# Key and query projections as three products of rounded high and low parts

## The chip, the cores and the metric

The kernel runs on one core of a Trainium2 chip. The metric is the device time of one execution in microseconds (us). The profile has five engines: TensorE (PE, with its weight loads as PEld), VectorE (DVE), ScalarE (ACT), GpSimd (POOL) and SyncE (SP), which only issues transfers here.

## The reference, cut to what matters

Two blocks of cross attention, a small mixture of experts and a quantised feed-forward layer, over 128 sequences of 64 tokens with 128 channels, 16 heads of 8 channels:

```python
x = x + tanh(g_xattn[0]) * L0_xattn(layernorm(x), ctx_1024, ctx_1024, ...)
x = x + tanh(g_ffn[0])   * L0_ffn(layernorm(x), ...)          # 4 experts, gated per token
x = x + tanh(g_xattn[1]) * L1_xattn(layernorm(x), ctx_1024, ctx_1024, mask, ...)
x = x + tanh(g_ffn[1])   * L1_ffn(layernorm(x), ...)          # quantised, depthwise convolution

# inside each xattn, all in float32:
q = query @ Wq.T + bq ; k = key @ Wk.T + bk ; v = value @ Wv.T + bv
attn = softmax(q k^T / sqrt(8)) ; out = (attn v) @ Wo.T + bo
```

## The kernel before, in words

**Tiles and groups.** A tile is two sequences, 128 rows; there are T = 64 tiles, and the residual stream `x_all` stays in SBUF. Four tiles make a group (G = 4); what comes ahead of the scores is done once per group with 512 columns. The stages follow one another: attention of layer 0 (L = 0), experts, attention of layer 1 (L = 1), feed-forward.

**One step of attention.** Each engine runs its own loop over the steps t (`attention(L)` on each engine, L442 on GpSimd, and the functions of the same name on the others), with j = t mod 4 the place in the group. `run_tiles` writes the first 8 and the last few steps out and loops over the rest, 8 steps to a body; in written-out steps t is a Python integer, in the loop a register. A step mixes the work of several tiles, and each engine takes its instructions in this order, so that the order written is the schedule; semaphores bind the engines. In step t:

- TensorE: scores of tile t (in layer 1 products that put in the mask first; both wait until VectorE has subtracted the maxima of tile t-1, `sub_done`), `values` of t-2, `transpose_p` first half of t-1, `transpose_o` of t-3 (waits for `x_attn`, the residual of t-4), then one piece of front work by j, then `transpose_p` second half, `project_o` of t-3. `bank[PT]` is one bank for both halves of `transpose_p`; ScalarE must have copied the first before the second is written.
- Front work by j, all in `bank[FRONT]`: j = 3 transposes the normalised queries of group (t+5)/4, j = 0 projects K (L1315), j = 1 projects Q (L1318), j = 2 projects V (L1323).
- ScalarE: exponentials second half of t-1, `copy_p` first half of t-1 (L581), `copy_o` of t-3, exponentials first half of t, `copy_p` second half of t-1, then the copy of the front work: `copy_xn` at j = 3 (L593), `copy_k` at j = 0 (L596), `copy_q` at j = 1 (L599), `copy_v` at j = 2.
- VectorE: residual of t-4 (L891), LayerNorm statistics of t+12 (L918), row maxima of the scores of t (`smax`, L923), the aggregate of the statistics (L925), two subtractions of the maxima (`prob`, L932), then `divide` of t-2 (`rden` L897, `o_n` L900).
- GpSimd: at j = 0 the scale and shift of the group t+8 (L382), at j = 0 and 1 its normalisation (L406, L408), at j = 1, 2, 3 the expansions of K for the scores (`expand_k`, L411), in every step the output bias onto `x_all` (L444).

**Types.** The K and Q projections of before are float32 matmuls with 128 rows, 128 weight columns and 512 moving columns; the profile shows two weight loads and two matmuls for one. The experts and the convolution already use the scheme of three products: an operand is copied to a rounded type (`F32R`, high part), the rest is the difference to it (low part), and high x high + high x low + low x high is added up (L1427 to L1429). For experts ScalarE makes the high part of the normalised tokens (L675) and VectorE the low (`split_mx`, L1042). GpSimd makes the low part of the convolution's weights (`tap_lower`, L515).

**Queues.** SyncE loads the context `ctx_t` of a group when V of the group two before is done, into two buffers; this is not touched.

Of the kernel before, what the change touches and what calls it, by code (L numbers as in the profile page):

```python
# [14 lines left out]
P = 128  # L15
# [11 lines left out]
G = 4  # L27
# [18 lines left out]
def build(nc, a, out):  # L46

    with ExitStack() as ctx:
# [3 lines left out]
        def sem(name):  # L52
# [134 lines left out]
            k_mm k_ready kj_ready v_mm v_ready q_mm q_ready  # L187
# [113 lines left out]
        RELU_A = tuple(c for c in range(EC) if c not in RELU_V)  # L301

# [72 lines left out]
        def _(pool):  # L375
# [47 lines left out]

            def attention(L):
                def step(t, k, has):
# [8 lines left out]
                    if j > 0 and has(f):  # L434
# [5 lines left out]
                        for h in ((), (0,), (1,), (2, 3))[j]:  # L440
                            expand_k(1 - gpar, h)
                    if has(0):  # L442
# [69 lines left out]
            def tap_lower():  # L512
# [7 lines left out]
            run_tiles(pool, attention(0), 8, 0, first=0, before={  # L520
                T - 8: lambda: lead_in(experts, -3, -3, NG), T - 7: lambda: lead_in(experts, -2, -2, NG)}, **TILES8)
# [5 lines left out]
                1: tap_scales, 4: lambda: tap_weights(0), 6: lambda: tap_weights(1), 7: lambda: tap_weights(2)}, **TILES8)  # L527
# [36 lines left out]
        def _(act):  # L564
# [27 lines left out]
            def copy_xn(src):  # L592
                act.activation(xn_t[:], src, ACT.Copy).then_inc(s["xn_copied"], G)  # L593
# [16 lines left out]
            def attention(L, beside=()):  # L610
                beside = dict(beside)

                def step(t, k, has):
# [12 lines left out]
                    if j == 3 and has(5):  # L626
                        f = n + 5
                        wait(act, "xn_tr", f + G)
                        wait(act, "q_mm", f)
                        copy_xn(bank[FRONT])  # L630
# [113 lines left out]
            def first_groups():  # L744
# [9 lines left out]
                copy_xn(bank[PT])  # L754
# [11 lines left out]
                copy_xn(bank[FRONT])  # L766
# [5 lines left out]
                T - 2: lambda: (normalise(1, 1, (2, 3)), relu(0, 0, 0, bank[FRONT]))}), 5, 0, first=0, before={  # L772
                T - 8: lambda: scale_wo(1), T - 5: lambda: split_weights(0), T - 4: lambda: split_weights(1)}, **TILES8)
# [54 lines left out]
            def attention1_tail():  # L828
# [16 lines left out]
            run_tiles(act, attention1, 5, 0, first=0, before={  # L845
                T - 8: lambda: copy_tap(0), T - 7: lambda: copy_tap(1), T - 5: lambda: (copy_tap(2), normalise_tile(0)),
# [7 lines left out]
        def _(dve):  # L854
# [49 lines left out]
            def attention(L):  # L904
                def step(t, k, has):
# [30 lines left out]
                    if has(-2):  # L936
                        divide(n - 2, k)
                return step
# [335 lines left out]
        def _(pe):  # L1274
# [44 lines left out]

            def project_v(L, gp, dst):  # L1320
# [7 lines left out]
            def attention(L, beside=()):  # L1328
                beside = dict(beside)

                def step(t, k, has):
# [32 lines left out]
                    if j == 0 and has(4):  # L1364
                        pe.wait_ge(ctx_ld[1 - gpar], group_loads(n + 4, 1 - gpar))
                        wait(pe, "xn_copied", n + 4 + G)
                        project_k(L, 1 - gpar, bank[FRONT])
                    if j == 1 and has(3):
                        wait(pe, "k_ready", n + 3 + G)
                        project_q(L, bank[FRONT])  # L1370
# [337 lines left out]
```

## Time and profile before

| | |
|---|---|
| median of 3 runs | 1009.33 us (999.88 to 1013.99) |
| the profiled execution, timed | 1009.39 us |
| its span | 1007.6 us |
| instructions | 36351 |
| granted TensorE clock, mean | 0.988 |
| moved between HBM and the core | 21.49 MB, 21 GB/s |

The span goes from the first to the last instruction on the core; 1.8 us of the timed execution lie around it. Busy time of an engine leaves out register, branch and semaphore instructions. Matmuls are pipelined: one shown as 0.40 us can be followed by the next after 0.23 us, so that a busy TensorE is not one at its peak. The idle time of an engine is put down to what ended it (after `<-`). A row of busy time by window gives the stretch, its length, the busy us (x instructions) of PE, PEld, DVE, ACT and POOL in this order, then the granted clock, the DMA share and GB/s.

### The profile page before, as it was taken

How to read it: one execution, taken by the hardware profiler on the slowest of the kernel's cores; microseconds unless marked ns; L12 is line 12 of the kernel's file. 1: busy time of each engine (PE TensorE's matmuls, PEld its weight loads, DVE VectorE, ACT ScalarE, POOL GpSimd, SP SyncE). 2: the span in 40 equal slices, each digit the busy share in tenths (PEclk: the TensorE clock that was granted, in tenths of full speed). 3: DMA queues.
4: the chain of work that ended last, by engine and by line, in shares of the span. 5: the costliest groups of instructions: out<-in, count | busy, mean ns of one | idle time of the engine just before them, and what ended most of it. 6: DMA issues, size and time to landing. Idle time of an engine off the chain costs nothing.

```text
span 1007.6 us, 36351 instructions
## 1 busy us (share of the span) xinstructions
PE 958.8 (95%) x11842; PEld 743.9 (74%) x11842; DVE 846.0 (84%) x2411; ACT 741.9 (74%) x1653; POOL 584.5 (58%) x1230
## 2 busy tenths in 40 slices
PE   6999999999999999999999999999999899999997
PEld 2777777777789999998877676767776666777775
DVE  5888888889689989888887888888877789999997
ACT  4877787788687777775657777777778777777774
POOL 6454554545125556656886535454554288888884
PEclk9999999999699999999999999999999999999999
DMA  3401010100000000000000000000000000000001
GB/s 108 176 24 42 21 42 31 32 21 11 13 2 2 0 0 0 0 0 1 2 12 24 13 22 10 21 10 12 19 11 2 2 15 21 21 21 21 21 21 30
DMA packets 19359, 21.49 MB, mean 21 GB/s; under 512 B 3552, under 2 KB 12000, under 8 KB 19296
## 3 DMA queue, kind: packets, MB, share of 16 engines
q1 hardware_dynamic: 19296, 20.68, 6.6%
q8 instruction: 35, 0.57, 0.2%
q14 instruction: 28, 0.23, 0.1%
HBM read 16.48 MB, written 4.19 MB: 21 GB/s over the span
## 4 chain that ended last, share of the span: by engine, by line
PE 30%; POOL 13%; issue 7%; ACT 2%; DVE 1%; POOLq 1%; ACTq 0%; DVEq 0%
PE bank L1276 8%; PE bank L1299 6%; POOL ln_rs L271 4%; PE score L1353 4%; POOL hid_b L555 3%; PE bank L1414 2%; PE score L1345 2%; PE bank L1323 2%; POOL xdq L551 2%; PE bank L1315 1%; PE bank L1311 1%; PE bank L1318 1%; ACT prob_t L581 1%; POOL ln_nr L271 1%; POOL ln_ve L271 1%
## 5 line engine op out<-in xcount | busy, mean ns | idle before, releaser
L581 ACT ACTIVATE prob_t<-bank 128x512 f32<-128x512 f32 x256 | 152.8, 597 | 124.9 <-PE bank L1276 116.8
L923 DVE TENSOR_REDUCE smax<-score 128x16 f32<-128x1024 f32 x128 | 156.8, 1225 | 49.1 <-PE score L1353 38.0
L1276 PE MATMUL bank<-const,prob 128*128 128x128 f32 x1024 | 167.7, 287 | 15.7 <-ACT prob_t L581 15.7
L1299 PEld LDWEIGHTS bank<-vb,prob_t 128*64 128x64 f32 x4096 | 131.6, 139 | 50.3 <-issue 42.2
L932 DVE TENSOR_TENSOR prob<-score,smax 128x512 f32<-128x512 f32 x256 | 164.9, 686 | 1.3
L576 ACT ACTIVATE prob<-prob 128x512 f32<-128x512 f32 x256 | 161.2, 630 | 6.1 <-DVE prob L932 5.4
L1276 PEld LDWEIGHTS bank<-const,prob 128*128 128x128 f32 x1024 | 109.4, 142 | 69.9 <-issue 60.7
L1299 PE MATMUL bank<-vb,prob_t 128*64 128x18 f32 x4096 | 144.4, 213 | 0.0
L411 POOL TENSOR_SCALAR kj<-k_sb,const 128x512 f32<-128x512 f32 x128 | 88.1, 695 | 74.8 <-issue 46.3
L656 ACT ACTIVATE eb_t<-eb,gwt 128x128 f32<-128x128 f32 x256 | 81.4, 390 | 45.2 <-POOL eb_acc L454 29.0
L382 POOL TENSOR_TENSOR a_ve<-a_mv,const 128x4 f32<-128x4 f32 x32 | 6.5, 203 | 147.9 <-DVE a_mv L925 143.8
L1353 PE MATMUL score<-kj,q_sb 32*64 32x256 f32 x2048 | 90.4, 409 | 1.8 <-ACT q_sb L599 0.9
L1555 PE MATMUL score<-f_wk_hi,tap_hi 128*128 128x512 f32 x192 | 81.8, 426 | 1.9 <-issue 1.8
L1556 PE MATMUL score<-f_wk_lo,tap_hi 128*128 128x512 f32 x192 | 75.7, 394 | 0.0
L1557 PE MATMUL score<-f_wk_hi,tap_lo 128*128 128x512 f32 x192 | 75.6, 394 | 0.0
L1414 PE MATMUL bank<-ew,hid_b 128*128 128x128 f32 x512 | 64.1, 280 | 2.5 <-DVE hid_b L1020 2.5
L1414 PEld LDWEIGHTS bank<-ew,hid_b 128*128 128x128 f32 x512 | 62.1, 196 | 4.5 <-issue 2.8
L1414 PE MATMUL bank<-ew,hid_a 128*128 128x128 f32 x512 | 62.8, 276 | 0.5 <-DVE x_all L1031 0.5
L1414 PEld LDWEIGHTS bank<-ew,hid_a 128*128 128x128 f32 x512 | 60.8, 192 | 3.0 <-DVE x_all L1031 0.9
L891 DVE TENSOR_TENSOR x_all<-bank,x_all 128x128 f32 (+1 forms) x128 | 37.2, 290 | 29.3 <-PE bank L1311 26.9
L444 POOL TENSOR_TENSOR x_all<-x_all,bo_row 128x128 f32 (+1 forms) x128 | 58.1, 457 | 0.0
L470 POOL TENSOR_TENSOR m_ve<-m_mv,const 128x4 f32<-128x4 f32 x16 | 3.3, 203 | 90.1 <-DVE m_mv L1054 86.1
(157 smaller groups left out, 2378.7 us busy)
## 6 DMA issues: line engine op xcount, KB each, us to landing
ctx_t<-in_ctx SPq DMA_DIRECT2D x32, 256.0 KB, 2.6
x_all<-in_x SPq DMA_DIRECT2D x16, 256.0 KB, 2.8
out_x<-x_all SPq DMA_DIRECT2D x64, 64.0 KB, 1.5
ew<-in_ew SPq DMA_DIRECT2D x2, 512.0 KB, 5.8
f_cw<-in_f_cw SPq DMA_DIRECT2D x1, 768.0 KB, 7.7
w_t<-in_w_attn SPq DMA_DIRECT2D x2, 256.0 KB, 3.8
f_w<-in_f_w SPq DMA_DIRECT2D x2, 256.0 KB, 6.5
eb<-in_L_ffn_eb SPq DMA_DIRECT2D x1, 256.0 KB, 6.5
```

The costliest lines, as they stand in the source:

```text
L411: pool.tensor_scalar(kj[:, gp, h, :], k_sb[:], const[:, C_J + h:C_J + h + 1], 0.0, ALU.mult, ALU.add).then_inc(s["kj_ready"], 1)
L576: act.activation(v, v, ACT.Exp, scale=SCALE).then_inc(s["exp_done"], 1)
L581: act.activation(prob_t[:, 4 * half:4 * half + 4, :].rearrange("p i q -> p (i q)"), bank[PT], ACT.Copy).then_inc(s["p_copied"], 1)
L656: act.activation(eb_t[:, j % 2, e, :], eb2[:, e * P:(e + 1) * P], ACT.Copy, scale=gwt[:, gp, j, e:e + 1]).then_inc(s["eb_mult"], 1)
L923: dve.tensor_reduce(smax[:].rearrange("p (r h) -> p r h", r=RH), sc, AX.X, ALU.max).then_inc(s["smax_done"], 1)
L932: dve.tensor_tensor(prob[:, par, half * 512:(half + 1) * 512].rearrange("p (r h k) -> p r h k", r=2, k=S), sc[:, g], m.unsqueeze(3).to_bro ...
L1276: return pe.transpose(dst, src, ident)
L1299: last = pe.matmul(bank[OV][q, i * 2 * VW:(i + 1) * 2 * VW], prob_t[:, i, q], vb[:, k // G, v0 + b * NPAIR + i, :, :].rearrange("p h v -> ...
L1353: last = pe.matmul(bank[r][q, 0:SW], q_sb[c, gpar, g], kj[c, gpar, :, g], start=(L == 0), stop=True, skip_group_check=True)
L1414: last = pe.matmul(bank[6 + j % 2][:, e * P:(e + 1) * P], hid[gpar][:, 2 * e + c, j * P:(j + 1) * P], ew2[:, 2 * e + c, :], start=(c == 0) ...
L1555: pe.matmul(bank[par], hi, f_wk_hi[:, tap, :], start=(tap == 0), stop=False)
L1556: pe.matmul(bank[par], hi, f_wk_lo[:, tap, :], start=False, stop=False)
```

## The change

Where K and Q are projected, the 512-column float32 product is replaced by three products of rounded operands, in every group but the first two of each layer (`whole(t, ...)` keeps these as they were). The high and low parts are formed thus:

- context: GpSimd multiplies `ctx_t` by one into `ctx_hi` and subtracts for `ctx_lo` (`split_ctx`), in its step j = 3, behind `expand_k` and ahead of the output bias. It waits for the loaded context, the K projection before, and its own high part.
- normalised queries: ScalarE's `copy_xn` writes the rounded `xn_hi` in place of `xn_t`; VectorE subtracts `xn_hi` from `bank[FRONT]` into `xn_lo`, at the end of its step j = 3, behind `divide`, waiting for `xn_copied`.
- weights: once per layer, ScalarE copies Wq and Wk to `w_hi` ahead of step 2, GpSimd subtracts for `w_lo` ahead of step 3.

TensorE waits for `ctx_lo_done` and `xn_lo_done` ahead of K. The parts lie in buffers of the experts and of the convolution that are free in attention, so no SBUF is added. The V projection stays float32 and reads `ctx_t`.

```diff
@@ -184,7 +184,7 @@
             tanh_done ident16_done wo_scaled setup_v mask_v vb_set thr_done zero_set edges_set
             sum_mm ffn_sum tern cw_scaled tap_ready tap_copied tap_split w2t_copied
             a_ln a_mean a_ready a_scaled a_xn_ready xn_tr xn_copied
-            k_mm k_ready kj_ready v_mm v_ready q_mm q_ready
+            k_mm k_ready kj_ready v_mm v_ready q_mm q_ready ctx_hi_done ctx_lo_done xn_lo_done w_hi_done w_lo_done
             scores_mm smax_done sub_done exp_done
             p_tr p_copied pv_mm rden_done o_norm o_tr o_copied wo_mm bo_added x_attn
             ln ln_mv ln_ready xn_ready
@@ -299,6 +299,19 @@
         GATE_STEPS = 16
         RELU_V = (1, 3, 7)
         RELU_A = tuple(c for c in range(EC) if c not in RELU_V)
+
+        ctx_hi, ctx_lo = mx_hi[:, 0, :], mx_lo[:, 0, :]
+        xn_hi, xn_lo = mx_hi[:, 1, :], mx_lo[:, 1, :]
+        w_hi = f_wk_hi[:, TAPS - 1, 0:2 * P].rearrange("p (w d) -> p w d", w=2)
+        w_lo = f_wk_lo[:, TAPS - 1, 0:2 * P].rearrange("p (w d) -> p w d", w=2)
+
+        def whole(t, first):
+
+            return isinstance(t, int) and t <= first
+
+        def parts_done(L, n):
+
+            return n - G - 2 * G * L
 
         block = ctx.enter_context(nc.Block())
 
@@ -421,6 +434,20 @@
                 for j in range(2):
                     normalise_pair(G, G, j)
 
+            def split_ctx(L, n, gp):
+                in_registers(pool, n, parts_done(L, n))
+                pool.wait_ge(s["const_in"], 16)
+                pool.wait_ge(ctx_ld[gp], group_loads(n, gp))
+                wait(pool, "k_mm", n)
+                pool.tensor_scalar(ctx_hi, ctx_t[:, gp, :], const[:, C_ONE:C_ONE + 1], 0.0, ALU.mult, ALU.add)\
+                    .then_inc(s["ctx_hi_done"], G)
+                wait(pool, "ctx_hi_done", parts_done(L, n))
+                pool.tensor_tensor(ctx_lo, ctx_t[:, gp, :], ctx_hi, ALU.subtract).then_inc(s["ctx_lo_done"], G)
+
+            def split_qk_weights(L):
+                pool.wait_ge(s["w_hi_done"], L + 1)
+                pool.tensor_tensor(w_lo, w_t[:, L, 0:2, :], w_hi, ALU.subtract).then_inc(s["w_lo_done"], 1)
+
             def attention(L):
                 def step(t, k, has):
                     n = L * T + t
@@ -439,6 +466,8 @@
                         wait(pool, "scores_mm", n + f - G)
                         for h in ((), (0,), (1,), (2, 3))[j]:
                             expand_k(1 - gpar, h)
+                    if j == 3 and has(5) and not whole(t, -1):
+                        split_ctx(L, n + 5, gpar)
                     if has(0):
                         wait(pool, "a_xn_ready", n + 1)
                         pool.tensor_tensor(x_tile(t), x_tile(t), bo_row[:, L, :], ALU.add)\
@@ -518,13 +547,14 @@
             first_groups()
             pool.wait_ge(s["setup_v"], 1)
             run_tiles(pool, attention(0), 8, 0, first=0, before={
+                3: lambda: split_qk_weights(0),
                 T - 8: lambda: lead_in(experts, -3, -3, NG), T - 7: lambda: lead_in(experts, -2, -2, NG)}, **TILES8)
             run_tiles(pool, experts, 3, 1, T=NG, first=-1, before={
                 NG - 3: lambda: (lead_in(attention1, -8, -5, mod=8), ternary(f_w1[:], 0)),
                 NG - 2: lambda: ternary(f_w2[:].rearrange("p c d -> p (c d)"), 1)})
             pool.wait_ge(s["setup_v"], 2)
             run_tiles(pool, attention1, 8, 0, first=0, before={
-                1: tap_scales, 4: lambda: tap_weights(0), 6: lambda: tap_weights(1), 7: lambda: tap_weights(2)}, **TILES8)
+                1: tap_scales, 3: lambda: split_qk_weights(1), 4: lambda: tap_weights(0), 6: lambda: tap_weights(1), 7: lambda: tap_weights(2)}, **TILES8)
 
             def ffn(t, par, has):
 
@@ -589,8 +619,12 @@
                                ACT.Identity, bias=b_col[:, L, 2:3])\
                     .then_inc(s["o_copied"], 1)
 
-            def copy_xn(src):
-                act.activation(xn_t[:], src, ACT.Copy).then_inc(s["xn_copied"], G)
+            def split_qk_weights(L):
+                act.wait_ge(s["w0_in" if L == 0 else "w1_in"], 16)
+                act.activation(w_hi, w_t[:, L, 0:2, :], ACT.Copy).then_inc(s["w_hi_done"], 1)
+
+            def copy_xn(src, dst):
+                act.activation(dst, src, ACT.Copy).then_inc(s["xn_copied"], G)
 
             def copy_k(L, src):
                 act.activation(k_sb[:], src, ACT.Identity, bias=b_col[:, L, 1:2]).then_inc(s["k_ready"], G)
@@ -627,7 +661,7 @@
                         f = n + 5
                         wait(act, "xn_tr", f + G)
                         wait(act, "q_mm", f)
-                        copy_xn(bank[FRONT])
+                        copy_xn(bank[FRONT], xn_t[:] if whole(t, -1) else xn_hi)
                     if j == 0 and has(4):
                         f = n + 4
                         wait(act, "k_mm", f + G)
@@ -751,7 +785,7 @@
                 act.wait_ge(s["k_mm"], G)
                 copy_k(0, bank[FRONT])
                 act.wait_ge(s["xn_tr"], G)
-                copy_xn(bank[PT])
+                copy_xn(bank[PT], xn_t[:])
                 act.wait_ge(s["q_mm"], G)
                 copy_q(0, 0, bank[OW])
                 act.wait_ge(s["g_in"], 32)
@@ -763,13 +797,14 @@
                 act.wait_ge(s["vb_set"], 3)
                 copy_v(0, bank[OV])
                 act.wait_ge(s["xn_tr"], 2 * G)
-                copy_xn(bank[FRONT])
+                copy_xn(bank[FRONT], xn_t[:])
 
             first_groups()
             run_tiles(act, attention(0, {
                 T - 7: lambda: normalise(0, 0, (0, 1)), T - 6: lambda: normalise(0, 0, (2, 3)),
                 T - 5: lambda: copy_mx(0, 0), T - 3: lambda: normalise(1, 1, (0, 1)),
                 T - 2: lambda: (normalise(1, 1, (2, 3)), relu(0, 0, 0, bank[FRONT]))}), 5, 0, first=0, before={
+                2: lambda: split_qk_weights(0),
                 T - 8: lambda: scale_wo(1), T - 5: lambda: split_weights(0), T - 4: lambda: split_weights(1)}, **TILES8)
             attention0_tail()
             run_tiles(act, experts, 2, 1, T=NG, first=1)
@@ -843,6 +878,7 @@
                 copy_xq(3, 1)
 
             run_tiles(act, attention1, 5, 0, first=0, before={
+                2: lambda: split_qk_weights(1),
                 T - 8: lambda: copy_tap(0), T - 7: lambda: copy_tap(1), T - 5: lambda: (copy_tap(2), normalise_tile(0)),
                 T - 4: lambda: (clear_edges(), normalise_tile(1)), T - 3: lambda: (quantise(0, 0), normalise_tile(2)),
                 T - 2: lambda: (quantise(1, 1), normalise_tile(3)), T - 1: copy_w2}, **TILES8)
@@ -935,6 +971,10 @@
                                 .then_inc(s["sub_done"], 1)
                     if has(-2):
                         divide(n - 2, k)
+                    if j == 3 and has(5) and not whole(t, -1):
+
+                        wait(dve, "xn_copied", n + 5 + G)
+                        dve.tensor_tensor(xn_lo, bank[FRONT], xn_hi, ALU.subtract).then_inc(s["xn_lo_done"], G)
                 return step
 
             def gate(ins):
@@ -1316,6 +1356,11 @@
 
             def project_q(L, dst):
                 pe.matmul(dst, w_t[:, L, 0, :], xn_t[:], start=True, stop=True).then_inc(s["q_mm"], G)
+
+            def project_parts(w, hi, lo, name):
+                pe.matmul(bank[FRONT], w_hi[:, w, :], hi, start=True, stop=False)
+                pe.matmul(bank[FRONT], w_hi[:, w, :], lo, start=False, stop=False)
+                pe.matmul(bank[FRONT], w_lo[:, w, :], hi, start=False, stop=True).then_inc(s[name], G)
 
             def project_v(L, gp, dst):
                 for i in range(G * BT):
@@ -1362,12 +1407,23 @@
                     if isinstance(t, int) and t in beside:
                         beside[t]()
                     if j == 0 and has(4):
-                        pe.wait_ge(ctx_ld[1 - gpar], group_loads(n + 4, 1 - gpar))
-                        wait(pe, "xn_copied", n + 4 + G)
-                        project_k(L, 1 - gpar, bank[FRONT])
+                        f = n + 4
+                        if whole(t, 0):
+                            pe.wait_ge(ctx_ld[1 - gpar], group_loads(f, 1 - gpar))
+                            wait(pe, "xn_copied", f + G)
+                            project_k(L, 1 - gpar, bank[FRONT])
+                        else:
+                            if isinstance(t, int):
+                                pe.wait_ge(s["w_lo_done"], L + 1)
+                            wait(pe, "ctx_lo_done", parts_done(L, f))
+                            wait(pe, "xn_lo_done", parts_done(L, f))
+                            project_parts(1, ctx_hi, ctx_lo, "k_mm")
                     if j == 1 and has(3):
                         wait(pe, "k_ready", n + 3 + G)
-                        project_q(L, bank[FRONT])
+                        if whole(t, 1):
+                            project_q(L, bank[FRONT])
+                        else:
+                            project_parts(0, xn_hi, xn_lo, "q_mm")
                     if j == 2 and has(2):
                         wait(pe, "q_ready", n + 2 + G)
                         project_v(L, 1 - gpar, bank[FRONT])
```

## Rows read from the trace of the kernel before

**Rows 1.** The page: busy time, share of the span and instructions of each engine

```profile
PE 958.8 (95%) x11842; PEld 743.9 (74%) x11842; DVE 846.0 (84%) x2411; ACT 741.9 (74%) x1653; POOL 584.5 (58%) x1230
```

**Rows 2.** Busy time by window: one group in layer 0, one in layer 1

```profile
98.21:114.50 16.29, 15.93 (x292) 11.89 (x276) 13.96 (x32) 12.99 (x27) 8.48 (x17) 1.00 0.11 32
...
604.87:622.25 17.38, 17.06 (x294) 12.34 (x292) 14.27 (x32) 12.89 (x26) 8.32 (x16) 1.00 0.05 15
```

**Rows 3.** Timeline (start us, us, engine), layer 0, the tile of a Q projection

```profile
104.09 1.02 PE L1318 MATMUL bank<-xn_t,w_t 128*128 128x512 f32 x2
...
104.24 0.60 ACT L581 ACTIVATE prob_t<-bank 128x512 f32<-128x512 f32 x1 [0.78 <-PE bank L1276]
...
104.95 0.42 PEld L1276 LDWEIGHTS bank<-const,prob 128*128 128x128 f32 x4 [0.67 <-issue]
```

**Rows 4.** Timeline, layer 0, from step j = 3 to the next tile

```profile
113.79 0.29 DVE L900 TENSOR_TENSOR o_n<-bank,rden 128x128 f32<-128x128 f32 x1
...
114.49 0.59 ACT L593 ACTIVATE xn_t<-bank 128x512 f32<-128x512 f32 x1
114.50 0.29 DVE L891 TENSOR_TENSOR x_all<-bank,x_all 128x128 f32 x1 [0.42 <-PE bank L1311]
...
115.41 1.23 DVE L923 TENSOR_REDUCE smax<-score 128x16 f32<-128x1024 f32 x1 [0.22 <-DVE a_st L918]
...
116.37 1.02 PE L1315 MATMUL bank<-ctx_t,w_t 128*128 128x512 f32 x2
...
118.21 0.69 PE L1353 MATMUL score<-kj,q_sb 32*64 32x256 f32 x16 [0.16 <-DVE prob L932]
...
118.56 0.29 DVE L891 TENSOR_TENSOR x_all<-bank,x_all 128x128 f32 x1
...
119.26 1.23 DVE L923 TENSOR_REDUCE smax<-score 128x16 f32<-128x1024 f32 x1 [0.21 <-DVE a_st L918]
```

**Rows 5.** Timeline, expert stage, TensorE: one product in three parts

```profile
402.01 0.48 PE L1427 MATMUL score<-mx_hi,ew_hi 128*128 128x512 f32 x1
402.33 0.40 PE L1428 MATMUL score<-mx_lo,ew_hi 128*128 128x512 f32 x1
402.56 0.39 PE L1429 MATMUL score<-mx_hi,ew_lo 128*128 128x512 f32 x1
```

**Rows 6.** Timeline, expert stage: the split of the normalised tokens

```profile
384.29 0.58 ACT L675 ACTIVATE mx_hi<-bank 128x512 fp32r<-128x512 f32 x1
...
384.91 0.69 DVE L1042 TENSOR_TENSOR mx_lo<-bank,mx_hi 128x512 fp32r<-128x512 f32 x1 [0.22 <-ACT mx_hi L675]
385.52 0.21 DVE L986 TENSOR_REDUCE g_rank<-g_gt 128x16 f32<-128x64 f32 x1
```

**Rows 7.** GpSimd: one line's instructions (ns min/median/max); timeline, layer 1, shortest hole

```profile
L515 POOL TENSOR_TENSOR f_wk_lo<-hid_b,f_wk_hi x3: 1270/1277/1279, 774.5 to 776.9; 128x512 fp32r<-128x512 f32 x3
...
533.40 0.20 POOL L382 TENSOR_TENSOR a_ve<-a_mv,const 128x4 f32<-128x4 f32 x1 [2.88 <-DVE a_mv L925]
```

**Rows 8.** Timeline: query copies and next scores or masks, first and last

```profile
33.71 0.59 ACT L593 ACTIVATE xn_t<-bank 128x512 f32<-128x512 f32 x1
...
37.21 0.66 PE L1353 MATMUL score<-kj,q_sb 32*64 32x256 f32 x12
...
243.98 0.59 ACT L593 ACTIVATE xn_t<-bank 128x512 f32<-128x512 f32 x1
...
247.39 0.47 PE L1353 MATMUL score<-kj,q_sb 32*64 32x256 f32 x8
...
535.53 0.59 ACT L593 ACTIVATE xn_t<-bank 128x512 f32<-128x512 f32 x1
...
539.36 0.39 PE L1345 MATMUL score<-neg_mask,ident 64*128 64x256 bf16 x4
...
761.38 0.59 ACT L593 ACTIVATE xn_t<-bank 128x512 f32<-128x512 f32 x1
...
765.21 0.39 PE L1345 MATMUL score<-neg_mask,ident 64*128 64x256 bf16 x4
```

## Prediction

> **What bounds the kernel now.** I read the busy times first, then the steady groups of both attention layers, then the order of events inside one tile. Over the span TensorE shows 95% matmul time, VectorE 84%, ScalarE 74%, GpSimd 58%, and the weight-load row 74% [rows 1]. That looks like a TensorE kernel, and a change that takes matmul passes away looks right. In one group of four tiles the picture is closer: of 16.29 us in layer 0 VectorE works 13.96, in layer 1 14.27 of 17.38; GpSimd works about half [rows 2]. So VectorE has 2.33 and 3.11 us free per group, in small pieces, and everything depends on where a new VectorE instruction falls.
>
> The chain inside a tile decides. In the tile of a query projection the two instructions of the projection start at 104.09 and the next transposes load at 104.95, which is 0.86 us; but ScalarE's copy of the first four transposed probabilities runs from 104.24 to 104.84, and the transposes need that bank [rows 3]. The wait for the copy ends within 0.11 us of the load, as it would with no projection there. The projection therefore already lies beneath this copy.
>
> The other place is the seam between the tile that transposes the normalised queries (j = 3) and the next. VectorE ends `o_n` at 114.08, adds the residual at 114.50, takes the maxima from 115.41, and subtracts; TensorE's next scores at 118.21 wait for that subtraction. ScalarE copies the transposed queries only from 114.49 to 115.08, last thing in its step [rows 4]. Maxima to next scores is 118.21 - 115.41 = 2.80 us.
>
> **TensorE's part.** The new K and Q projections are three products. Nearest rows are the expert products, the same shapes and types: starts at 402.01, 402.33, 402.56 and one of 0.39 to 0.48 us each [rows 5]. So an isolated triple takes 0.32 + 0.23 + 0.39 = 0.94 us to its end, against 1.02 for the present pair, and gives the array back after 0.32 + 0.23 + 0.23 = 0.78 us against at most 0.86 [rows 3, 5]. If the first gap were 0.23 too, it is 0.69. Between 0.08 and 0.17 us is saved, 2 x 14 times per layer, 56 in all: 4.5 to 9.5 us of array time. I credit nothing: in the Q tile the copy holds the transposes, and in the K tile, by the part below, TensorE waits longer for VectorE. Without that cover the 4.5 to 9.5 us would count.
>
> The Trainium skill, "Perfetto Trace Analysis", section "Identifying the Most-Contended Engine", says that matmul busy time does not measure TensorE's headroom and that weight-load share and other engines' occupancy should be used. By that rule VectorE and not TensorE is the contended engine here, the change adds work to it, and the 4.5 to 9.5 us are not there; by the page of the profile's 95% they would be. The copy row bears the rule out.
>
> **ScalarE's part.** The copy of the transposed queries goes to another buffer in the rounded type; the same copy with a rounded output takes 0.58 us against 0.59 [rows 4, 6]. Nothing. The weights' high part is one 128x256 copy per layer, bounded by nothing and by a 128x512 copy of 0.59 us; ScalarE has 3.3 us free per group [rows 2]. Zero, at most 2 x 0.6 = 1.2 us.
>
> **GpSimd's part.** Per group it gets one subtraction 128x512 from two SBUF operands, 1.28 us, and one scaled copy 128x512, between nothing and the same 1.28 us since it reads one operand less; I take the upper end, 2.6 us together [rows 7]. They stand behind the last expansions of K and ahead of one bias addition that is used four tiles later, and ahead of the next group's statistics. Before those GpSimd waits for VectorE's means; the shortest such hole in the 28 groups is 2.88 us, in the first of layer 1 [rows 7]. There the low part of the weights (a 128x256 subtraction, between nothing and 1.28 us) is added: 2.6 + 1.3 = 3.9 at most, 1.0 over, but the normalised tiles are not transposed for two more tiles. The K projection that needs the parts is a whole tile and more behind. Cost zero; if the cover were gone, 28 x 2.6 = 73 us would be the upper bound, which half-idle GpSimd [rows 2] makes remote. The context loads are two groups ahead and aren't moved.
>
> **VectorE's part, which carries the sum.** `xn_lo` is a 128x512 subtraction with one PSUM operand. Its twin `mx_lo` takes 0.69 us, the instruction behind it starts 0.61 us after it, and it starts 0.04 us after ScalarE's copy ends (384.29 + 0.58 = 384.87, start 384.91) [rows 6]. Its place is the end of step j = 3, behind `o_n`, and it waits for `xn_copied`. Behind it in VectorE's order are the residual, the LayerNorm statistics, and the maxima of the next tile, for which TensorE's scores wait. Counted from the start of the copy of the queries:
>
> - copy ends at 0.59; `xn_lo` starts at 0.63; VectorE had been free since 114.08 - 114.49 = -0.41, so it first stands still for 1.04 us [rows 4, 6];
> - the residual starts at 0.63 + 0.61 = 1.24 instead of 0.01;
> - residual to maxima is 119.26 - 118.56 = 0.70 where nothing else holds it [rows 4]: maxima at 1.94;
> - maxima to next scores 2.80: the scores start 4.74 after the copy starts.
>
> Before, these scores (or the mask products ahead of them in layer 1) start after 3.50 us in the first group of layer 0 and 3.41 in the last, 3.72 in the group shown, with a mean of 3.54 over the 14; in layer 1 after 3.83 in the first and last, mean 3.84 over 14 [rows 4, 8]. The seam grows by 4.74 - 3.54 = 1.20 us and by 4.74 - 3.84 = 0.90 us. Everything of the next tile hangs on those scores and comes later by the same amount: values, transposes, copies, then again scores. The tiles between are held by TensorE and the copies, so that later tiles can't win it back. 14 x 1.20 + 14 x 0.90 = 16.8 + 12.6 = 29.4 us. The first two groups of each layer are projected whole and don't pay.
>
> The Trainium skill, "TensorE: Matmul & The Clock Gate", section "Architectural detail", says that VectorE and ScalarE take their queues strictly in order. By that rule the ready residual can't pass the waiting subtraction. If it could, the wait would cost nothing and only the length of the instruction would count, which is the second rival.
>
> **The sum.** The profiled execution is 1007.6 us long and was timed at 1009.4, next to the median of 1009.3. 1009.4 + 29.4 = 1038.8: I predict 1039 us, 2.9% slower. Its own range is 1028 to 1050: the seam's terms are off by at most 0.2 us each way for two of the sums (the 0.91 from residual to maxima at 114.50 instead of 0.70 gives 28 x 0.21 = 6 more; the uncredited array time gives up to 9.5 less), the weights up to 1.2 more, and the runs before spread by some 5 us about their median.
>
> **Rivals.**
> 1. *TensorE is the bound after all and VectorE takes the new work in its gaps.* For it: 95% busy [rows 1], 2.3 us free per group [rows 2]. It would need the copy of the queries to end before VectorE's `o_n` does; it ends 1.00 us after it, in order behind a probability copy [rows 4]. It decides if VectorE's lateness at the seam stays under TensorE's own 0.08 to 0.17 us gains. Then 1009.4 - 4.5 to 9.5: 1002 us, no slowdown. Chance 0.05.
> 2. *Only the length counts, not the wait.* The scheduling shifts so that the copy comes earlier or the residual gets ahead. Then the residual starts 0.61 later than its natural -0.41 + 0.42 = 0.01 at worst, and the scores 0.01 + 0.61 + 0.70 + 2.80 = 4.12 after the copy: 14 x 0.58 + 14 x 0.28 = 12 us, 1021 us. Or the delay is won back in part where VectorE now waits for scores. Against it: the copy and the residual are each in program order. Chance 0.14.
> 3. *Something else gets late besides.* TensorE's transpose of `o_n` waits for the residual, and it is the instruction just ahead of the K projection, which starts 116.37 - 114.49 = 1.88 us after the copy. The residual of the seam would now end at 1.24 + 0.29 = 1.53 [rows 4]: a cover of some 0.2 us. GpSimd's pair could also delay K's expansion or the means. One more 0.5 us per group is 28 x 0.5 = 14: 1053 us. Chance 0.13.
>
> The forecast itself has 0.68. Range for 8 in 10: 1020 to 1052, which takes in the middle of rival 2 and the edge of rival 3. Faster by over 2%: 0.03 (rival 1 with more than its own gain). Within 2%, up to 1029.5, about what a measurement of this kernel can tell from no change: 0.19 (the rest of rival 1, most of rival 2, the low edge of the forecast). Slower: 0.78.
>
> **What would show it.** In the profile after: VectorE's idle time before `xn_lo` released by ScalarE's `xn_hi` copy, near 1.0 us x 28, and 28 x 0.69 us of work; 4.7 us from that copy to the next scores; the idle time before the probability copy in ScalarE and before scores in TensorE grown in one tile of four; K and Q triples of about 0.94 us; GpSimd's hole before the means shorter by 2.6 us at most, and its statistics no later after the means. Expert and convolution stages unchanged. If `xn_lo` shows little idle time before it, or the tile after it is no longer than its neighbours, the central step is wrong.

## The result, and the profile after

| | before | changed |
|---|---|---|
| median, 6 runs each | 1001.45 us (999.88 to 1013.99) | 1039.35 us (1033.36 to 1046.23) |
| ratio, 95% interval | | 1.034 (1.029 to 1.039) |
| span of the profiled execution | 1007.6 us | 1033.1 us |

The change makes the kernel 3.4% slower. Here and below, ratios are taken over the executions less than 1.5% above their kernel's fastest and are not the quotients of the medians, which here give 1.038. The page's line of busy times, to be laid beside [rows 1]:

```profile
PE 952.8 (92%) x11898; PEld 751.9 (73%) x11898; DVE 859.9 (83%) x2439; ACT 741.8 (72%) x1655; POOL 640.0 (62%) x1288
```

TensorE works 6 us less and VectorE 14 us more, and neither number is the loss. One group of four tiles in each layer, in the columns of [rows 2]:

```profile
104.51:121.77 17.26, 15.78 (x292) 12.34 (x278) 14.49 (x33) 12.87 (x26) 10.19 (x19) 1.00 0.12 31
621.76:640.00 18.24, 17.05 (x297) 12.65 (x297) 14.80 (x33) 12.88 (x27) 10.16 (x19) 1.00 0.06 14
```

A group is longer by 1.0 and 0.9 us than those of [rows 2] (1.1 and 0.9 if both are counted from copy to copy; the groups next to these, behind a seam of 5.1 us, grow by 1.4 and 1.3). VectorE works only 0.5 more in it, and no engine is full. So it is a wait. The list of waits of the changed kernel has one that before has not (us in total, times, longest):

```profile
DVE mx_lo L977 <- ACT mx_hi L627: 29.9, 28, 1.4
```

That is `xn_lo` behind ScalarE's copy `xn_hi` (both live in the experts' buffers and show their names). The timeline of the seam, VectorE and ScalarE, in layer 0, answers to [rows 4]:

```profile
121.17 0.29 DVE L936 TENSOR_TENSOR o_n<-bank,rden 128x128 f32<-128x128 f32 x1
...
121.77 0.59 ACT L627 ACTIVATE mx_hi<-bank 128x512 fp32r<-128x512 f32 x1
...
122.47 0.69 DVE L977 TENSOR_TENSOR mx_lo<-bank,mx_hi 128x512 fp32r<-128x512 f32 x1 [1.00 <-ACT mx_hi L627]
...
123.18 0.29 DVE L927 TENSOR_TENSOR x_all<-bank,x_all 128x128 f32 x1
...
123.57 0.29 DVE L954 BATCH_NORM_STATS2 a_st<-x_all 128x6 f32 x1
...
124.09 1.23 DVE L959 TENSOR_REDUCE smax<-score 128x16 f32<-128x1024 f32 x1 [0.23 <-DVE a_st L954]
```

VectorE is done with `o_n` at 121.46 and stands until the copy has ended at 122.36. The maxima, which followed 0.92 us after the start of the copy, now follow 2.32 us after it (124.09 - 121.77). TensorE in the same tile, where the new K projection stands:

```profile
123.63 0.47 PE L1361 MATMUL bank<-mx_hi,f_wk_hi 128*128 128x512 f32 x1
123.94 0.39 PE L1362 MATMUL bank<-mx_lo,f_wk_hi 128*128 128x512 f32 x1
124.17 0.40 PE L1363 MATMUL bank<-mx_hi,f_wk_lo 128*128 128x512 f32 x1
124.54 0.63 PE L1316 MATMUL bank<-const,prob 128*128 128x128 f32 x4
125.01 0.39 PE L1351 MATMUL bank<-w_t,o_t 128*128 128x128 f32 x2
126.88 0.69 PE L1398 MATMUL score<-kj,q_sb 32*64 32x256 f32 x16 [1.49 <-DVE prob L968]
```

The projection runs as the experts' triple did [rows 5], 0.94 us to its end. It starts 1.86 us after the start of the copy, where it was 1.88 [rows 4], so TensorE's new waits ahead of K cost nothing here. Behind the output projection TensorE then waits 1.49 us for the subtraction of the maxima, the largest gap it has in the tile, and starts the scores 5.11 us after the copy instead of 3.72. Over the whole kernel these waits are, before and then changed:

```profile
PE score L1345 <- DVE prob L932: 1.5, 1, 1.5
PE score L1353 <- DVE prob L932: 0.7, 4, 0.2
```

```profile
PE score L1398 <- DVE prob L968: 16.6, 15, 1.5
PE score L1390 <- DVE prob L968: 13.0, 15, 1.5
```

From the scores (or mask products) of tile 0 to those of tile 56 the changed kernel takes 246.9 us in layer 0 and 255.7 in layer 1, before 226.2 and 243.2: 33 us more in the 28 seams and the groups behind them, 2.7 of them by TensorE's clock (section on the clock).

### The profile page after: what moved, and what is told of

It reads as the page before. It is cut to its first block, busy times and chain, and to the rows that moved or that the text cites. A ratio compares the mean times of both kernels' runs of the same rounds, so it can differ in the third digit from the quotient of the medians.

```text
span 1033.1 us, 36641 instructions
## 1 busy us (share of the span) xinstructions
PE 952.8 (92%) x11898; PEld 751.9 (73%) x11898; DVE 859.9 (83%) x2439; ACT 741.8 (72%) x1655; POOL 640.0 (62%) x1288
## 4 chain that ended last, share of the span: by engine, by line
PE 23%; POOL 12%; issue 10%; DVE 3%; ACT 3%; DVEq 0%; POOLq 0%; ACTq 0%
PE bank L1316 6%; PE bank L1339 5%; POOL ln_rs L271 4%; PE score L1398 3%; POOL hid_b L585 2%; PE bank L1470 2%; PE bank L1368 2%; POOL xdq L581 2%; PE score L1390 2%; ACT prob_t L611 1%; POOL ln_nr L271 1%; DVE prob L968 1%; POOL ln_ve L271 1%; DVE smax L959 1%; POOL ln_nm L271 1%
## 5 line engine op out<-in xcount | busy, mean ns | idle before, releaser
L1398 PEld LDWEIGHTS score<-kj,q_sb 32*64 32x64 f32 x2048 | 30.7, 131 | 42.1 <-issue 37.3
```

The lines of the kernel that those rows point to most:

```text
L1398: last = pe.matmul(bank[r][q, 0:SW], q_sb[c, gpar, g], kj[c, gpar, :, g], start=(L == 0), stop=True, skip_group_check=True)
```

## Experiments: each part by itself

Three kernels hold one part of the change each. Edits are shown against the changed kernel, cut to what matters. Times of before beside them: median 1001.67 us, 999.2 to 1012.8 over 19 executions.

**VectorE's part alone** (`e1_vector_alone`):

```diff
-                            project_parts(1, ctx_hi, ctx_lo, "k_mm")
+                            project_k(L, 1 - gpar, bank[FRONT])      # K waits for xn_lo_done; Q whole too
-                    if j == 3 and has(5) and not whole(t, -1):       # GpSimd: no split_ctx, no weight parts
-                        split_ctx(L, n + 5, gpar)
+                        dve.tensor_tensor(xn_lo, bank[FRONT], xn_t[:], ALU.subtract)
```

> The kernel before with nothing of the change but VectorE's subtraction at the end of its step j = 3 and the K projection's wait for it; the projections stay whole float32, nobody reads the difference. My theory (VectorE stands still for ScalarE's copy, and the next tile's maxima and scores come late): the copy of the queries to the next scores takes 4.7 to 5.1 us in place of 3.5 to 3.9, and 28 such seams cost 30 to 36 us, some 1032 to 1040 where before takes 1002. Rival (the three products or GpSimd's pair carry a good part of the loss): less than 20 us over before.

Measured 1036.98 us (1034.47 to 1042.09), ratio 1.033 (1.025 to 1.041). The wait is there, with the same size:

```profile
DVE mx_lo L972 <- ACT xn_t L624: 30.6, 28, 1.4
```

The seam, from the copy to the next scores, lasts 4.85 us on average in layer 0 and 4.73 in layer 1, to a hundredth what the changed kernel has. One instruction in 28 places is the slowdown, within what these runs tell.

**GpSimd's part alone** (`e2_gpsimd_alone`): as above, but with `split_ctx` and without VectorE's subtraction; K waits for `ctx_lo_done`.

> The kernel before with nothing of the change but GpSimd's two instructions per group (high and low part of the context) and the K projection's wait for them; the parts are not used, the projections stay whole float32. My theory: within 3 us of before, since GpSimd does it in its wait for VectorE's means, which shrinks from 5.3 to about 3.3 us. Rival (GpSimd becomes late, or its traffic slows VectorE): 10 us or more over before, or VectorE's instructions longer than 0.69 and 1.23 us while GpSimd works.

Measured 1006.41 us (1000.18 to 1014.31), ratio 1.004 (0.999 to 1.009). The seams last 3.54 and 3.84 us, as before, and the 56 tiles of either attention take 226.2 and 243.2 us, as before. The pair is hidden. The statistics in one group of before, and then one such pair and the statistics behind it in the changed kernel:

```profile
112.37 0.20 POOL L382 TENSOR_TENSOR a_ve<-a_mv,const 128x4 f32<-128x4 f32 x1 [5.29 <-DVE a_mv L925]
```

```profile
114.72 1.28 POOL L445 TENSOR_TENSOR mx_lo<-ctx_t,mx_hi 128x512 fp32r<-128x512 f32 x1 [0.16 <-POOL mx_hi L442]
...
119.75 0.20 POOL L395 TENSOR_TENSOR a_ve<-a_mv,const 128x4 f32<-128x4 f32 x1 [3.33 <-DVE a_mv L961]
```

3.33 of the hole's 5.29 us are left. The median is 5 us above that of before because several of its ten executions had a lower granted clock (see below); those at 0.993 or more took 1000.2 to 1001.4 us.

**TensorE's part alone** (`e3_tensor_alone`; GpSimd and ScalarE still make the high parts, and K and Q wait for those only):

```diff
-                        dve.tensor_tensor(xn_lo, bank[FRONT], xn_hi, ALU.subtract)...
-                pool.tensor_tensor(ctx_lo, ctx_t[:, gp, :], ctx_hi, ALU.subtract)...
-                            project_parts(1, ctx_hi, ctx_lo, "k_mm")
+                            project_parts(1, ctx_hi, ctx_hi, "k_mm")     # Q likewise
```

> The three products alone: VectorE's subtraction and GpSimd's are left out, and the high part stands in for the low one in the second product, so the small correction by the operands' low parts is not what is computed. My theory: nothing gained on TensorE, since the next transposes wait for ScalarE's copy: within 3 us of before. Rival (TensorE is the bound and the shorter projections count): 4.5 to 9.5 us faster than before.

With the high part in the second product too, K and Q come out about doubled, which is more than the expectation says; the time does not depend on it. Measured 1009.36 us (998.98 to 1022.33), ratio 0.998 (0.993 to 1.004). Its executions at a clock of 0.995 or more took 999.0 to 1003.0 us, those of before 999.2 to 1003.2. The profile shows why nothing is won; the tile of a Q projection, to compare with [rows 3]:

```profile
103.33 0.48 PE L1355 MATMUL bank<-mx_hi,f_wk_hi 128*128 128x512 f32 x1
...
103.56 0.60 ACT L609 ACTIVATE prob_t<-bank 128x512 f32<-128x512 f32 x1 [0.78 <-PE bank L1310]
103.64 0.39 PE L1356 MATMUL bank<-mx_hi,f_wk_hi 128*128 128x512 f32 x1
...
103.88 0.40 PE L1357 MATMUL bank<-mx_hi,f_wk_lo 128*128 128x512 f32 x1
...
104.27 0.42 PEld L1310 LDWEIGHTS bank<-const,prob 128*128 128x128 f32 x4 [0.44 <-issue]
```

The third product could be followed after 0.23 us, at 104.11. The transposes load at 104.27, again 0.11 us after the end of the copy (104.16). The shorter projection ends in front of the same wait.

## Experiments: the length and the wait

**The subtraction twice** (`e7_subtract_twice`), the first into a buffer nobody reads:

```diff
+                        dve.tensor_tensor(f_wk_lo[:, 0, :], bank[FRONT], xn_hi, ALU.subtract)
                         dve.tensor_tensor(xn_lo, bank[FRONT], xn_hi, ALU.subtract)...
```

> The changed kernel with VectorE's subtraction done twice in a row, the first into a buffer that nobody reads. My theory: the place of the instruction is on the chain of the seam, so each second one adds its whole 0.61 us: 28 x 0.61 = 17 us over the changed kernel, some 1056 us, and the seam grows from 4.7 to 5.1 to 5.3 to 5.7 us. Rival (VectorE has room there, only the wait counts): within 5 us of the changed kernel's 1039.

Measured 1056.15 us (1052.97 to 1061.08), 16.8 above the changed kernel's median, ratio to before 1.049 (1.041 to 1.058). The seams grew from 4.85 to 5.30 and from 4.73 to 5.16 us, 28 x 0.44 = 12 us, not 17. The added work is on the chain, but not with its whole length: the first of the two starts 0.07 us earlier than the one did, 0.53 us are left, and in every second seam a part covers something else that stood there (section on the loop's turn). That the time came out as expected is luck. Between the profiled executions lie 26.2 us (spans 1059.3 and 1033.1): 12 in the seams, and most of the rest in TensorE's clock, which in this one fell to half behind six seams, not two, and for 17 us from about 290 on.

**ScalarE's copy earlier** (`e5_early_copy`): the lines with `copy_xn` moved ahead of `exponentials(n, par, 0)` and `copy_p(n - 1, 1)` in ScalarE's step.

> The changed kernel with ScalarE's copy of the transposed queries taken ahead of the exponentials and the second probability copy of its step; nothing else is changed. My theory: the copy ends about when VectorE finishes o_n, the idle time before the subtraction falls from 1.0 us to near nothing, and only the length is paid: seams longer than before by 0.1 to 0.6 us, 5 to 14 us over before, near 1011. Rival (ScalarE's order is as tight, exponentials and probability copies come 0.5 us late): 14 to 25 us over before.

Measured 1006.76 us (1001.79 to 1022.76), ratio 1.004 (1.000 to 1.009). All work of the change is still done. The seam, here counted from the start of `o_n` (113.79 in both):

```profile
113.18 0.60 ACT L627 ACTIVATE mx_hi<-bank 128x512 fp32r<-128x512 f32 x1
113.79 0.29 DVE L936 TENSOR_TENSOR o_n<-bank,rden 128x128 f32<-128x128 f32 x1
114.00 0.68 DVE L977 TENSOR_TENSOR mx_lo<-bank,mx_hi 128x512 fp32r<-128x512 f32 x1
...
114.60 0.29 DVE L927 TENSOR_TENSOR x_all<-bank,x_all 128x128 f32 x1
...
115.52 1.22 DVE L959 TENSOR_REDUCE smax<-score 128x16 f32<-128x1024 f32 x1 [0.23 <-DVE a_st L954]
```

`xn_lo` follows `o_n` without idle time, the residual starts 0.10 us later than in [rows 4], and the maxima 0.11. The 56 tiles take 228.0 and 243.4 us, 1.7 and 0.3 over before; I had expected 5 to 14. In this seam 0.42 of the 0.61 us lie in time in which VectorE used to wait for TensorE's output projection [rows 4]. So with the operand there in time, all but 2 of some 31 us are gone. That does not price the wait by itself: behind a late copy the length counts too, as the doubled subtraction shows.

**Behind the statistics** (`e4_behind_stats`): the subtraction moved into VectorE's step j = 0, behind the residual and the statistics, ahead of the maxima.

> The changed kernel with VectorE's subtraction moved behind the residual and the statistics of the next step, ahead of the maxima; the same work, the same result. ScalarE's copy is then over before VectorE arrives. My theory: the wait of 1.0 us goes, and of the 0.61 us some 0.4 to 0.6 stay in layer 0 (maxima follow the statistics at once) and 0.1 to 0.4 in layer 1, where VectorE waits for scores: 8 to 13 us over before, near 1012. Rival (VectorE's added work as such costs, wherever it stands): as the changed kernel, near 1038.

Measured 1011.43 us (1008.12 to 1020.91), ratio 1.009 (1.005 to 1.013). In every second seam of the loops the copy is over before VectorE comes:

```profile
117.31 0.59 ACT L627 ACTIVATE mx_hi<-bank 128x512 fp32r<-128x512 f32 x1
117.41 0.29 DVE L927 TENSOR_TENSOR x_all<-bank,x_all 128x128 f32 x1 [0.42 <-PE bank L1351]
...
118.02 0.68 DVE L957 TENSOR_TENSOR mx_lo<-bank,mx_hi 128x512 fp32r<-128x512 f32 x1
118.61 1.21 DVE L963 TENSOR_REDUCE smax<-score 128x16 f32<-128x1024 f32 x1
```

In the others VectorE is there sooner and still waits, mostly about 0.3 us. Of the 29.9 us of waiting 7.0 are left:

```profile
DVE mx_lo L957 <- ACT mx_hi L627: 7.0, 19, 0.7
```

The seams are 4.02 us: 14 x (4.02 - 3.54) + 14 x (4.02 - 3.84) = 9 us, as expected. Most of the wait is gone, but the length stands where VectorE has little room. The same instruction costs 31, 9 or 2 us by its place and by when its operand is ready.

**GpSimd subtracts** (`e6_gpsimd_subtracts`): ScalarE copies the queries twice, rounded and in full, GpSimd forms `xn_lo` from the two in step j = 0, and only Q waits for it.

```diff
+                        act.activation(xn_hi, bank[FRONT], ACT.Copy)     # then copy_xn into xn_t
+                        pool.tensor_tensor(xn_lo, xn_t[:], xn_hi, ALU.subtract)...
-                            wait(pe, "xn_lo_done", parts_done(L, f))
+                            wait(pe, "xn_copied", f + G)
```

> The changed kernel with the low part of the queries made by GpSimd from two SBUF operands, for which ScalarE copies the queries a second time, in full; VectorE gets nothing, and only the Q projection waits for the low part. My theory: the seam goes back to 3.5 to 3.9 us (up to 0.3 more where the second copy of 0.5 us delays an exponential), within 5 us of before, near 1002. If the shorter products on TensorE are worth 4.5 to 9.5 us after all, this is the run that is faster than before. Rival (GpSimd with 1.28 us more per group gets late): over 1015.

Measured 1005.99 us (1000.10 to 1021.94), ratio 1.001 (0.996 to 1.006). The 56 tiles take 226.2 and 243.3 us, what they take before. The change as a whole, with its three products, can be had for nothing, and gives nothing in time. I found no version that beats the kernel before.

## Experiments: the loop's turn and the clock

In the changed kernel the seams of the loops alternate between about 4.69 and 5.11 us. The turn of VectorE's 8-step loop lies in every second one. `e9_loop_offset` starts this loop two steps later in layer 1 (`lo=10` for VectorE alone), so that it turns elsewhere.

> The changed kernel with VectorE's loop of layer 1 begun two steps later, so that the turn of its 8-step body falls between j = 1 and j = 2 and no longer into a seam (j = 3 to j = 0). In the changed kernel every other seam has the residual 0.1 and the statistics 0.2 us later and lasts 5.1 us in place of 4.7 from the copy to the next scores. Theory (the turn of VectorE's loop, hidden before the change, lies bare on the chain there): in layer 1 all seams of the loop last 4.7 us. Rival (a two-buffer effect that alternates with the groups): seams of 4.7 and 5.1 us go on alternating.

From the third group of layer 1 to the twelfth all ten seams are 4.69 or 4.70 us. The same seam in the changed kernel, and then in this one:

```profile
640.69 0.69 DVE L977 TENSOR_TENSOR mx_lo<-bank,mx_hi 128x512 fp32r<-128x512 f32 x1 [1.00 <-ACT mx_hi L627]
641.38 0.29 DVE L927 TENSOR_TENSOR x_all<-bank,x_all 128x128 f32 x1
641.80 0.29 DVE L954 BATCH_NORM_STATS2 a_st<-x_all 128x6 f32 x1
642.32 1.22 DVE L959 TENSOR_REDUCE smax<-score 128x16 f32<-128x1024 f32 x1 [0.23 <-DVE a_st L954]
```

```profile
640.37 0.69 DVE L977 TENSOR_TENSOR mx_lo<-bank,mx_hi 128x512 fp32r<-128x512 f32 x1 [1.07 <-ACT mx_hi L627]
640.98 0.28 DVE L927 TENSOR_TENSOR x_all<-bank,x_all 128x128 f32 x1
641.17 0.28 DVE L954 BATCH_NORM_STATS2 a_st<-x_all 128x6 f32 x1
641.67 1.23 DVE L959 TENSOR_REDUCE smax<-score 128x16 f32<-128x1024 f32 x1 [0.21 <-DVE a_st L954]
```

From the subtraction to the maxima it is 1.63 us with the turn and 1.30 without. Its one execution took 1033.8 us, within the spread; the reading rests on the profile. A longer subtraction covers part of the turn, which is why doubling it lengthened the seams with a turn by only 0.2 us (5.11 to 5.33) and those without by 0.53.

**The clock.** In the profile of the changed kernel TensorE's clock falls to half behind two seams of layer 0, at the first of them from about 57.7 us to 61:

```profile
54.00:55.00 1.00, 0.34 (x4) 0.15 (x2) 0.96 (x4) 0.06 (x1) 0.00 (x0) 1.00 0.00 0
55.00:56.00 1.00, 0.35 (x16) 0.27 (x16) 0.90 (x4) 1.00 (x3) 0.00 (x0) 1.00 0.00 0
...
57.00:58.00 1.00, 1.00 (x20) 0.97 (x16) 1.00 (x3) 0.15 (x1) 1.00 (x3) 0.86 0.00 0
58.00:59.00 1.00, 1.00 (x5) 0.81 (x4) 1.00 (x3) 0.81 (x3) 1.00 (x3) 0.50 0.00 0
59.00:60.00 1.00, 1.00 (x5) 0.80 (x4) 0.71 (x3) 0.56 (x2) 1.00 (x2) 0.50 0.00 0
...
62.00:63.00 1.00, 1.00 (x28) 0.97 (x25) 1.00 (x2) 0.23 (x1) 0.84 (x2) 1.00 0.00 0
```

(stretch, its length, busy of PE, PEld, DVE, ACT, POOL, then the clock.) TensorE worked 0.34 and 0.35 us of the two microseconds from 54 to 56, in the seam's wait, and was full again from 56 on; from 57.7 it ran at 1.2 GHz for 3.4 us and then at 2.4 again. The two groups with such a fall, 18.72 and 19.06 us from copy to copy, are 1.3 and 1.4 us longer than the same groups of the filled kernel below. The profile has three more stretches at half clock away from the seams: from 16 to 24 us, from 494 to 498 and in the last 6 us. `e8_filler` gives TensorE work in the seam: K's first product is written four times more.

```diff
+                            for _ in range(4):
+                                pe.matmul(bank[FRONT], w_hi[:, 1, :], ctx_hi, start=True, stop=True)
                             project_parts(1, ctx_hi, ctx_lo, "k_mm")
```

> The changed kernel with the first of K's three products written four times more ahead of the three (0.9 us more of TensorE's work per group, in the tile in which TensorE waits for VectorE). In the changed kernel's profile the granted clock fell to half twice in layer 0, each time right after a wait of TensorE of 1.3 to 1.5 us in this tile. Theory that the falls come from TensorE's idle time: no such fall in the attention of this kernel, mean clock 0.99 or more in every run, and a time at or below the changed kernel's, in spite of the added work. Rival (the falls have nothing to do with it): clocks between 0.979 and 0.994 as before, and the time the same or a few us longer.

> The changed kernel itself, unaltered, beside the next one and on the same chip, to compare their granted clocks over many runs. Its six runs so far took 1033 to 1046 us at mean clocks of 0.994 down to 0.979. Theory (the clock falls behind TensorE's wait in the seam): again a spread of 10 us or so with clocks between 0.979 and 0.994. Rival (that chip or hour had it, not the kernel): all runs near 1033 at 0.994.

> The changed kernel with the first of K's three products written four times more, as in the earlier filler run, whose four executions took 1033.6 to 1034.6 us at 0.995. Theory: every execution again at 0.99 or more and within 3 us of 1034, so that 0.9 us more of TensorE's work per group costs nothing and takes the spread away. Rival: the four steady executions were luck, and the spread is that of the changed kernel beside it.

`e10_changed_again` is the changed kernel, unaltered, and `e11_filler_again` the filled one once more. The filled kernel took 1034.45 us (1033.57 to 1034.62) in the first four executions, and in six more beside the changed kernel 1032.74 us (1031.50 to 1033.73), where the changed kernel took 1040.05 us (1033.21 to 1042.10). Its mean clock was 0.993 to 0.997 in all ten; the changed kernel's twelve executions had 0.979 to 0.994. In its seam TensorE waits half as long:

```profile
122.69 1.17 PE L1421 MATMUL bank<-mx_hi,f_wk_hi 128*128 128x512 f32 x4
...
125.95 0.69 PE L1398 MATMUL score<-kj,q_sb 32*64 32x256 f32 x16 [0.73 <-DVE prob L968]
```

0.9 us more of TensorE's work per group made the kernel 7 us faster at the median. The stretch between two seams is not shortened by it; the two profiled executions of the filled kernel have no fall behind a seam, that of `e10_changed_again` has one, and the best executions of the two kernels are within 2 us. Before has a fall at another place, and a longer one: its profiled execution ran for 17 us, from about 260 to 277, where layer 0 ends, at half clock. TensorE had worked 0.64 and 0.00 us of the two microseconds ahead of 260.

```profile
262.00:280.00 18.00, 17.33 (x192) 13.79 (x176) 11.39 (x25) 8.99 (x20) 0.00 (x0) 0.58 0.00 1
```

The changed kernel's profiled execution has no fall there. Near full clock before takes about 1001 us (15 of the 25 executions of one set lie between 999.9 and 1003.1), and the changed kernel 1033 at its highest clock of 0.994: 32 us apart.

## Why the prediction was right

It named 1039 us, 2.9% slower; 1039.35 us was measured, 3.4% slower. The mechanism stands: VectorE held by ScalarE's copy at the seam is where the time goes. The agreement to a microsecond does not mean as much: I worked from the profiled execution, 1009.4 us, where the median over six runs of before is 1001.45, and forecast 29.4 us of loss, where 37.9 lie between the medians. Two errors of 8 us cancel.

- **TensorE's saving credited at nothing: right.** The triple takes the time read off the experts, and TensorE's part alone is at 0.998. Rival 1 (TensorE is the bound) falls with that run and with the one in which GpSimd subtracts.
- **ScalarE's copies at nothing: right.** 0.59 us as before, and even a second one per group cost nothing.
- **GpSimd at nothing: right.** I took 2.6 us as the upper end for the pair; it is 0.69 + 0.16 + 1.28 = 2.1, and the hole before the means went from 5.3 to 3.3 us.
- **The wait of `xn_lo`: right in place and size.** 1.04 us forecast, 1.00 to 1.07 in most seams. In the seam shown it starts 0.11 us after the copy ends, not 0.04 as in the experts' row; why, no run shows (the first of the two subtractions of `e7_subtract_twice` starts 0.04 after it).
- **The seam: 4.74 us forecast; 4.69 without a loop turn and 5.11 with one.** Means 4.85 and 4.73. The term that was mis-sized is the 0.70 us from residual to maxima. [rows 4] held both values, 0.91 at 114.50 and 0.70 at 119.26, and I took the second as the rule and the first as an effect of waiting; it was the turn of the loop, bare on the chain in every second seam. Small errors offset each other beside it: the residual starts at 1.30 without a turn, not 1.24, and maxima to scores is then 2.69, not 2.80. By the trace 14 x 1.31 + 14 x 0.89 = 31 us, against 29.4.
- **Not won back later: right.** The tile behind the seam gets shorter by up to 0.35 us between maxima in layer 1, since the scores shift less than the maxima; counted at the scores, as the forecast did, nothing comes back.
- **Rival 2 (only the length counts):** priced at 12 us. Its condition holds in `e5_early_copy`, where the copy comes earlier; there it is 2 us, with most of the 0.61 us in time in which VectorE used to wait.
- **Rival 3 (something else late): not by way of GpSimd or the `o_n` transpose.** The transpose starts 1.83 us after the copy, 0.06 later than before at most, ahead of a TensorE that waits anyway. But something else did come: the granted clock, 2.7 us behind two seams of the profiled execution; the executions at 0.979 to 0.986 took 1039.6 to 1046.2 us, 6 to 13 above that at 0.994. The prediction had no term for it.
- **The base.** The page of before has one slice whose clock digit is 6 between nines. It was in front of me, and I priced nothing by it. The fall in it is some 7 us of the profiled execution: from the last seam of layer 0 to the first of layer 1 before takes 291.6 us, GpSimd's part alone, which has no fall there, 282.9, and 1.3 of the difference go to a short fall at 481. That is most of the gap between it and the shortest executions of before.

## What to carry to other kernels

An added instruction costs what its place costs: ask when its operand is ready and when its engine gets there, and what the engine would have done in between. Here the same subtraction on VectorE was 31, 9 or 2 us, and moved to GpSimd, where it is longer, nothing. Time saved on the busiest engine is worth nothing if it ends in front of the same wait, which one pair of rows (the copy's end, the next load's start) tells in advance. And look at the clock digits of the profiled execution before taking its time as the base of a sum.

## What the runs showed that I had not expected

- **TensorE's clock fell to half behind waits of 1.3 and 1.5 us.** Two such falls in the profiled execution, each for 3.4 us, each from some 2 us behind the end of a seam's wait; there are 28 seams, so most of them pass without one. With extra products in the gap no seam of the two profiled executions has a fall, all ten executions have mean clocks of 0.993 or more, and the median is 7 us lower. That the idle time is the cause rests on this pair of kernels; what separates a seam with a fall from one without is open, and so is why a fall lasts 3.4 us here and 17 us in the profile of before.
- **The turn of an 8-step loop on VectorE takes 0.3 to 0.4 us between the instructions around it,** and counts once it lies on the chain.
- **Three kernels of the same length in attention have medians up to 8 us apart:** before 1001.67, GpSimd's part 1006.41, TensorE's part 1009.36. At like clocks they agree: the executions at 0.995 or more took 999.0 to 1003.2 us in all three. Within one kernel, executions at 0.975 are 11 to 14 us longer than those at 0.996. Differences of less than 1% between such kernels are to be read from the stretches of the profile, not from medians of a few runs.
